# Layer 0 of a two-layer graph network: filter taps split four pairs at a time through device memory, one power for two roots, the gate kept in PSUM

## The reference

```
norm  = (sum(adj, -1) + 1e-6) ** -0.5
f_hom = norm * (adj @ (norm * (x @ theta)))
f_het = x @ W_h
gate  = sigmoid(x @ W_t + b_t)
x1    = layernorm(x + elu(gate * f_hom + (1 - gate) * f_het))
layer 1: conv1d(relu(bn(conv1d(x1, conv1_w))), conv2_w[256, 256, 17]), similarity message, GRU, layernorm
```

## Time and profile before

| | us |
|---|---|
| median of 3 runs (2112.98 to 2114.28) | 2113.04 |
| the profiled execution | 2112.74 |
| its span, first to last instruction | 2111.0 |
| `phase_a`: ends before the next phase's first instruction at | 541.60 |

### The profile page before, as it was taken

How to read it: one execution, slowest core, us unless ns; L and a number is a source line. 1 busy time by engine, 2 the same in 40 slices (tenths; PEclk the granted TensorE clock), 3 DMA queues, 4 the chain that set the end, 5 groups by cost and what they waited for, 6 DMA issues and landing times.

```text
span 2111.0 us, 36299 instructions
## 1 busy us (share of the span) xinstructions
PE 1916.6 (91%) x11046; PEld 1668.0 (79%) x11046; DVE 1551.1 (73%) x3024; ACT 1154.2 (55%) x2174; POOL 424.7 (20%) x374
## 2 busy tenths in 40 slices
PE   6888888888588879996699999999999999999997
PEld 5887777787588868885588888888888888888886
DVE  5998799898577767764577777777777777777774
ACT  6887688787355557664344444444444444444442
POOL 5887687686000000000000000000000000000000
PEclk9999999999699989998699999999999999999998
DMA  4565556565422238886212212121221212212110
GB/s 140 205 212 203 205 216 217 190 211 185 154 79 84 80 127 270 256 262 200 106 62 79 84 57 93 47 93 65 74 89 51 93 47 93 73 67 93 63 41 20
DMA packets 175099, 263.23 MB, mean 125 GB/s; under 512 B 13406, under 2 KB 125764, under 8 KB 170788
## 3 DMA queue, kind: packets, MB, share of 16 engines
q1 hardware_dynamic: 175012, 262.27, 36.7%
HBM read 174.14 MB, written 88.08 MB: 124 GB/s over the span
## 4 chain that ended last, share of the span: by engine, by line
PE 50%; issue 1%; DVE 1%; DMA 1%; SPq 0%; ACT 0%; POOLq 0%; POOL 0%; ACTq 0%; DVEq 0%
PE c_ps_g L1438 37%; PE c_ps_m L1416 4%; PE c_ps_m L1447 2%; PE c_ps_y L1473 1%; PE c_ps_m L1449 1%; PE c_ps_y L1531 1%; PE c_ps_m L1531 1%; PE c_ps_m L1448 1%; DMA c_yf<-y_spec 1%; PE c_ps_s L1516 0%; PE c_ps_y L1532 0%; PE c_ps_m L1532 0%; PE c_ps_s L1487 0%; PE c_ps_g L1490 0%; DVE c_wi_l L1381 0%
## 5 line engine op out<-in xcount | busy, mean ns | idle before, releaser
L1207 POOL TENSOR_TENSOR c_rstd<-c_var_eps,c_neg_half 128x4 f32<-128x4 f32 x32 | 32.2, 1007 | 1078.4 <-DVE c_var_eps L1345 1078.4
L1130 ACT ACTIVATE c_yo<-c_ps_y,c_shift,c_rstd 128x256 f32<-128x256 f32 x128 | 61.8, 563 | 170.0 <-DVE c_shift L1353 170.0
L1438 PE MATMUL c_ps_g<-c_ch,c_wi_l 128*128 128x512 f32 x384 | 154.6, 403 | 0.0
L1438 PE MATMUL c_ps_g<-c_nh,c_wi_l 128*128 128x512 f32 x384 | 153.3, 399 | 0.0
L837 PE MATMUL m_ps<-m_wh,m_xl 128*128 128x256 f32 (+1 forms) x406 | 132.9, 327 | 21.9 <-DVE m_wl L817 21.8
L1438 PE MATMUL c_ps_g<-c_xh,c_wh_l 128*128 128x512 f32 x384 | 152.1, 396 | 0.0
L1438 PE MATMUL c_ps_g<-c_xl,c_wh_h 128*128 128x512 f32 x384 | 152.0, 396 | 0.0
L1438 PE MATMUL c_ps_g<-c_xh,c_wh_h 128*128 128x512 f32 x384 | 151.7, 395 | 0.0
L1438 PE MATMUL c_ps_g<-c_ch,c_wi_h 128*128 128x512 f32 x384 | 151.6, 395 | 0.0
L1438 PE MATMUL c_ps_g<-c_cl,c_wi_h 128*128 128x512 f32 x384 | 151.6, 395 | 0.0
L1438 PE MATMUL c_ps_g<-c_nl,c_wi_h 128*128 128x512 f32 x384 | 151.2, 394 | 0.0
(11 more groups left out here) (225 smaller groups left out, 6403.8 us busy)
## 6 DMA issues: line engine op xcount, KB each, us to landing
w_spec<-a_spec SPq DMA_DIRECT2D x32, 1088.0 KB, 11.0
m_w<-w_spec SPq DMA_DIRECT2D x34, 1024.0 KB, 7.4
a_xt<-in_x_t SPq DMA_DIRECT2D x64, 256.0 KB
a_xn<-in_x_n SPq DMA_DIRECT2D x64, 256.0 KB, 9.5
x_t<-a_x1t SPq DMA_DIRECT2D x64, 256.0 KB, 9.8
s_x<-x_t SPq DMA_DIRECT2D x64, 256.0 KB, 3.0
y_spec<-m_y SPq DMA_DIRECT2D x64, 256.0 KB, 5.9
c_x<-x_t SPq DMA_DIRECT2D x32, 512.0 KB, 3.9
```

Source lines behind the costliest of these rows:

```text
L1130: nc.scalar.activation(yo[:, b], ps_y[:, b], ACT.Identity, bias=shift[:, b:b + 1], scale=rstd[:, b:b + 1]).then_inc(s_yo, 1)
L1207: nc.gpsimd.tensor_tensor(rstd[:, :], var_eps[:, :], neg_half[:, :], ALU.pow).then_inc(s_rstd, 1)
L1438: last = nc.tensor.matmul(out, stationary, moving, start=(count == 0), stop=(count == total - 1))
```

## The change

1. Taps. SP loads the taps of four pairs at once as a tile of 128 partitions (`tr`); ACT makes the high part `th` and DVE the low part `tl`, once in four steps. SP stores high, low and high to a new tensor in device memory, `taps_s`, and later loads for each pair one tile of 102 rows (`gs`, four buffers), already stacked. `gr`, `gh` and DVE's stacking go. The spectra of a pair are made four steps later than before (step q+6, the fourth one in q+7), and the quarters of `w_spec` are stored in steps n%8 = 1 to 4 and not 4 to 7; the last four follow the last step.
2. Roots. The sum of adj and the variance stand side by side in `sums_eps`, and POOL raises both to -0.5 in one instruction (`roots`). The addition of epsilon to the variance goes from ACT to DVE; `x1` becomes a `scalar_tensor_tensor` with the root broadcast as a second tensor.
3. Gate. The tanh is written back into `ps_g`; `gd` reads it there, and PE's next gate projection waits for `gd`. `mix` reads the second half of `ps_hh` and not `het`.
4. `xn` has four buffers; `res` stands ahead of `al` on POOL. On PE the projection of the first graph stands ahead of `ps_hom`. On DVE the statistics stand ahead of `diff`.
5. `phase_product` counts two semaphores in one.

```diff
 SP
-                    for copy in range(3):
-                        sp.dma_start(gr[copy * 2 * TAPS:(copy + 1) * 2 * TAPS, r].rearrange("p c k -> p (c k)"),
-                                     taps[:, bass.ts(i, 4 * P)]).then_inc(s_in[r], 16)
+                    if n % TB == 0:
+                        m = k * (UNROLL // TB) + n // TB
+                        reached(sp, s_tl, m)
+                        sp.dma_start(tr[:, :], here.rearrange("o p c -> (o p) c")).then_inc(s_tr, 16)
...
+                    if n % TB == 0:
+                        reached(sp, s_tl, m + 1)
+                        for copy, part in enumerate((th, tl, th)):
+                            sp.dma_start(here[:, copy].rearrange("o (p c) -> (o p) c", p=P), part[:, :].bitcast(F32)).then_inc(s_ts, 16)
+                if live(6):
+                    reached(sp, s_ts, 48 * (m + 1))
+                    sp.dma_start(gs[:, r].rearrange("p c k -> p (c k)").bitcast(F32),
+                                 here.rearrange("o h (r x c) -> (o h r) x c", x=TB, c=4 * P)[:, at_step]).then_inc(s_gs[r], 16)
-                piece = n % 8 - 4
-                if 0 <= piece < PIECES and live(5 + piece):
+                piece = n % 8 - 1
+                if 0 <= piece < PIECES and live(10 + piece):
 ACT
+                if live(7):
+                    spectra_out(i - 7, 3, 7)
...
-                    nc.scalar.activation(var_eps[:, :], mv[:, v, :, 1], ACT.Identity, bias=eps[:, 0:1]).then_inc(s_ve, 1)
-                    nc.scalar.activation(gate[:, u], ps_g[:, :, :], ACT.Tanh, scale=0.5).then_inc(s_gate, 1)
+                    nc.scalar.activation(ps_g[:, :, :], ps_g[:, :, :], ACT.Tanh, scale=0.5).then_inc(s_gate, 1)
 POOL
+                    nc.gpsimd.tensor_tensor(roots[:, u, these], sums_eps[:, u, these], neg_half[:, these], ALU.pow).then_inc(s_root, 1)
 DVE
-                    nc.vector.scalar_tensor_tensor(gd[:, :, :], gate[:, v], 1.0, diff[:, :, :], ALU.add, ALU.mult).then_inc(s_gd, 1)
+                    nc.vector.scalar_tensor_tensor(gd[:, :, :], ps_g[:, :, :], 1.0, diff[:, :, :], ALU.add, ALU.mult).then_inc(s_gd, 1)
-                        last = nc.vector.tensor_scalar(x1[:, u, b], y[:, u, b], mv[:, u, b, 0:1], rstd[:, u, b:b + 1],
+                        last = nc.vector.scalar_tensor_tensor(x1[:, u, b], y[:, u, b], mv[:, u, b, 0:1], roots[:, u, 2 + b:3 + b].to_broadcast([P, D]),
...
 PE
                 if live(2):
...
+                    project(0)
+                if live(7):
+                    spectra(i - 7, 3, 7)
...
-                    spectra(0)
-                    project(0)
-                    spectra(1)
+                if live(6):
+                    spectra(i - 6, 0, 6)
+                if live(2):
                     project(1)
...
-                    reached(pe, s_gate, p2)
+                    reached(pe, s_gd, p2)
```

More of the change, by code:

```diff
@@ L49, in pipeline, with phase_a @@
         step(i, i % unroll, i // unroll, lambda s, i=i: 0 <= i - s < units)
-def phase_a(nc, G, x_n, x_t, adj_t, w0, b_t, masks, x1_t, taps, dft_w, w_spec):
+def phase_a(nc, G, x_n, x_t, adj_t, w0, b_t, masks, x1_t, taps, taps_s, dft_w, w_spec):
     pairs = G // 2
@@ L130, in phase_a @@
         s_wl = sem("weights_low")
-        s_in = [sem(f"x_adj_taps_loaded{b}") for b in range(RING)]
-        s_xn = [sem("x_nodes_loaded0"), sem("x_nodes_loaded1")]
+        s_in = [sem(f"x_adj_loaded{b}") for b in range(RING)]
+        s_xn = [sem(f"x_nodes_loaded{b}") for b in range(RING)]
         s_xh = sem("x_high")
@@ L157, in phase_a @@
         s_ve = sem("var_eps_done")
-        s_rstd = sem("rstd_done")
         s_x1 = sem("x1_done")
-        s_tr = sem("transposed")
+        s_xp = sem("transposed")
         s_x1t = sem("x1t_copied")
         s_out = [sem("x1t_stored0"), sem("x1t_stored1")]
-        s_gh = sem("taps_high")
-        s_gs = sem("taps_stacked")
+        s_tr = sem("taps_loaded")
+        s_th = sem("taps_high")
+        s_tl = sem("taps_low")
+        s_ts = sem("taps_stored")
+        s_gs = [sem(f"taps_stacked{b}") for b in range(RING)]
         s_gm = sem("spectra_made")
@@ L364, in step @@
                     nc.vector.scalar_tensor_tensor(y[:, v], mix[:, v], 0.0, res[:, v], ALU.max, ALU.add).then_inc(s_y, 1)
-                if live(3):
-                    reached(dve, s_gd, p3)
-                    reached(dve, s_hom, p3 + 1)
-                    reached(dve, s_het, p3 + 1)
-                    for b in range(2):
-                        last = nc.vector.scalar_tensor_tensor(diff[:, b], ps_hom[:, b], norm[:, v, b:b + 1], het[:, v, b],
-                                                              ALU.mult, ALU.subtract)
-                    last.then_inc(s_diff, 1)
-                if live(5):
                     reached(dve, s_mv, p5)
@@ L390, in step @@
                 if live(3):
+                    reached(dve, s_gd, p3)
+                    reached(dve, s_hom, p3 + 1)
+                    reached(dve, s_het, p3 + 1)
+                    for b in range(2):
+                        last = nc.vector.scalar_tensor_tensor(diff[:, b], ps_hom[:, b], roots[:, v, b:b + 1], het[:, v, b],
+                                                              ALU.mult, ALU.subtract)
+                    last.then_inc(s_diff, 1)
+                if live(5):
+                    reached(dve, s_mv, p5 + 1)
+                    reached(dve, s_root, p5 + 3)
+                    nc.vector.scalar_tensor_tensor(sums_eps[:, v, 2:4], mv[:, v, :, 1], 1.0, eps[:, :], ALU.mult, ALU.add).then_inc(s_ve, 1)
@@ L486, in step @@
                     last.then_inc(s_gp, 1)
[L487 removed]
+                if live(6):
+                    spectra(i - 6, 2, 6)
             pipeline(pe, pairs, STAGES, step, unroll=UNROLL)
@@ L1647 @@
     y_n = nc.dram_tensor("out_y", (P, G * D), F32, kind="ExternalOutput").ap()
-    phase_a(nc, G, d["x_n"], d["x_t"], d["adj_t"], d["w0"], d["b_t"], d["masks"], x1_t, d["taps"], d["dft_w"], w_spec)
+    phase_a(nc, G, d["x_n"], d["x_t"], d["adj_t"], d["w0"], d["b_t"], d["masks"], x1_t, d["taps"], taps_s, d["dft_w"], w_spec)
     with ExitStack() as ctx:
```

196 lines of the change are left out of this document (98 added, 98 removed).

## The result

Median 2080.95 us (2077.3 to 2083.8, 4 runs) against 2113.66 (2112.98 to 2114.68, 4 runs): ratio 0.9844, 95% interval 0.9827 to 0.9861. The profiled execution took 2079.74 us, 33.0 less than before's 2112.74.

A forecast was written before the change was run, and what follows sets the result against it. It took two DMA engines loading the taps, then the engines' 7.55 us loop held by DVE, to bound the kernel. -5 - 5 - 44.6 - 1 + 15 = -40.6 took 2112.7 to 2072 us; range given 2048 to 2101.

The forecast's parts named there:

- start, to the gate of step 2: Kernel's beginning: ACT's first x no longer waits for the taps; -5 us (-3 to -7).
- steps 2 to 8: Six early steps of 7.15 us, four of them now without spectra, put at 6.3 each: -5 us (0 to -7).
- steps 8 to 63: Main stretch: 441.0 us becomes 55 x 7.0 + 11.4 = 396.4, so -44.6.
- steps 63 to 65: The last two steps take 14 us in place of 15.05: -1.
- end, to the next phase: Last four stores of spectra, 13.5 us in place of 4.3 (+9.2), and spectra through one buffer (+6): together +15.
- the step of 8.02: Mean step before, steps 8 to 63; explained by two DMA engines needing 6.5 us plain, 9.4 with a spectra store.
- The DMA sum of 8.0: Mean need per step of the two busiest DMA engines before: (6.5 + 9.4) / 2 = 8.0 us.
- the six engines that 102 rows were put at: Taps load at 17 rows to an engine: six DMA engines, 1.4 us; busiest engines then need 5.9 us a step.
- The rival of two engines: 102 rows still get two DMA engines: 8.7 us a step, main stretch 478.5, total 2155 us; chance 0.04.
- DVE falls off the path: Engines' loop of 7.55 us, held by DVE; edits change DVE's sum by -0.2 to -1.4 us, below what comes next.
- a ring of 7.0 us through ACT and PE: Gate, ACT's work and spectrum copy, then PE to the next gate: sum 6.9, taken as 7.0 us a step.
- The jumps back: Two loop ends where ACT's 4.27 us stall stays and PE's clock drops: 5.7 us each, 11.4 in all.

The follow-up runs named there:

- the two runs with the load's other form: Changed kernel with three loads of 34 rows: 2166.37 us, ratio 1.0259; kernel before with one load of 102 rows: 2088.66 us, ratio 0.9884.
- the extra operation: Changed kernel with one more 102x512 DVE operation in each step, the size of the removed `gs` stacking: 2080.84 us, ratio 0.9855.
- spectra off the ring: Changed kernel with PE's spectra and ACT's copies of them moved to where the buffer has long been free: 2075.92 us, ratio 0.9832.
- The runs with the start opened: Changed kernel, spectra moved, loop written out, PE's first step not waiting for `bt_rows`, 11 unneeded products ahead: 2052.12 us; also with two buffers for last three pairs' spectra: 2043.57.
- off the ring, no loop: Changed kernel with spectra and their copies moved to where the buffer is free, and all 64 steps written out: 2053.53 us, ratio 0.9729.
- stores two steps later: Changed kernel with the quarters of the spectra stored in steps n%8 = 3 to 6 in place of 1 to 4: 2077.42 us, ratio 0.9835.

## Why the prediction was right, and where it was off

By its own steps, in the profiled executions:

| step | predicted | measured |
|---|---|---|
| start, to the gate of step 2 | -5 | -1.0 (24.10, now 23.14) |
| steps 2 to 8 | -5 | -3.5 (42.90, now 39.37) |
| steps 8 to 63 | -44.6 | -40.8 (441.03, now 400.26) |
| steps 63 to 65 | -1 | -1.3 (15.05, now 13.74) |
| end, to the next phase | +15 | +16.9 (18.5, now 35.4) |
| the phases behind it | 0 | -3.7 (1569.4, now 1565.7) |
| sum | -40.6 | -33.4 |

The forecast of 2072 us was 9 too low, and by more in the part that changed: without the 3.7 us of the phases behind, which no run ties to the change, the gain would have been 29.7. That is luck on the forecast's side. So is a part of how the step of 8.02 was explained. The DMA sum of 8.0 contains no jump, but the measured mean does: 53 steps take 414.3 us, 7.82 each, with only eight of them over 9, and the two jumps 26.8. The cause named, the two engines, stands all the same by the two runs with the load's other form.

*The DMA engines* came out as worked out: the six engines that 102 rows were put at show in the share of 0.38 and held nothing up, while three loads of 34 rows behind the same stores did, in the same kernel. The rival of two engines (2155, with a main stretch of 478.5) was priced at about what that kernel then took (2166, 477.6).

*DVE falls off the path, and a ring of 7.0 us through ACT and PE comes next.* Both shown: the extra operation cost nothing, and spectra off the ring gave 6.82. The ring was the last to end by 0.16 us alone. Not shown is which edit took DVE off the path. PE's wait for `fl`, 0.84 us at a time before, is gone, and three things could have done it: the projection that now stands in front of `ps_hom`, the shorter `mix` and `gd`, and the `gs` that went. Only the last was put back by itself, and it didn't bring 7.55 back; no run undoes the order on PE or the operands in PSUM alone. `mix` at 688 ns is what the Trainium skill's "SBUF — State Buffer", section "Who interferes with whom", leads to for an operand moved to PSUM, and `gd` with 681 too; `x1`, which by that rule stays blocked, is not slower with its third input but faster than its 762, at 672. POOL's `res` fell as well, from 1724 to 1292 ns (60 to 215 us). But the prediction misread a row where it saw the rule confirmed: `gs`, with its 775 ns the unblocked one there, also has two SBUF inputs (`gh` and `gr`), and so has `y`, at 676 ns before and 688 after. Two inputs in SBUF don't make an operation slow by themselves, and no run moves one operand alone.

*The jumps back* were mis-sized: 11.4 for two, 15.7 measured. The step that failed was that the stall "stays". ACT's is the same, 4.46 us against 4.27 in the earlier trace rows, but DVE now stands twice. The timeline of the first jump:

```profile
228.59 0.16 DVE L379 TENSOR_SCALAR a_sums_eps<-a_ps_t 128x2 f32<-128x2 f32 x1 [4.61 <-issue]
228.95 0.63 ACT L269 ACTIVATE a_below<-a_mix 128x512 f32<-128x512 f32 x1 [4.46 <-issue]
...
233.88 0.18 DVE L392 BATCH_NORM_AGGREGATE a_mv<-a_stats 128x2 f32<-128x6 f32 x1 [3.25 <-issue]
```

The second jump is alike (4.51 and 3.15 on DVE). In the trace before DVE stood once, for 2.99 us in the first jump. The two jumps are 4.3 us over what was put down for them; the 53 other steps, (400.26 - 29.65) / 53 = 6.99 us each, give 0.4 of it back. That is all by which the main stretch missed. The runs show that the loop is what stalls, but not why DVE does so twice.

*The start* was the term furthest off. ACT did have its first x at 10.00, as said, but PE had something else to wait for, and then ran slowly. PE's first instruction in after, and two of its passes:

```profile
15.22 0.37 PE L472 MATMUL a_ps_t<-a_ones,a_al 128*128 128x2 f32 x1 [15.22 <-DVE a_bt_rows L370]
...
16.67 0.63 PE L463 MATMUL a_ps_hh<-a_w_lo,a_xh 128*128 128x512 f32 x1
...
21.29 0.39 PE L504 MATMUL a_ps_g<-a_bt_rows,a_ones 128*128 128x512 f32 x1
```

DVE's preparation of the weights ends in `bt_rows`, which nothing needs before the gate. The step to blame is that I followed ACT's wait and never asked what PE's first instruction waits for. Before, that was `al`, at 16.40, with `bt_rows` long done at 13.7; in after `bt_rows` itself ended only at 15.2, with DVE's `dw` at 1.50 us for 0.49 beside a POOL that now works at the same time. So PE began 1.2 us earlier, and not even that was kept whole: its passes became fast at 21.19 before and at 21.29 in after. The runs with the start opened give 2.2 us back, 4.5 where the passes were fast as well (gate at 19.47).

*Steps 2 to 8* were put at 6.3 us each. The four without spectra took that (6.25 to 6.35), the two with spectra 7.06 and 7.04: that is the missing 1.5.

*The end* was right in both terms. From the last copy of `x1t` at 497.50 the stores take to 511.90, where the next phase's first instruction stands:

```profile
497.50 0.60 ACT L305 ACTIVATE a_x1t<-a_ps_t 128x512 f32<-128x512 f32 x1 [0.45 <-PE a_ps_t L500]
...
511.90 0.20 POOL L597 MEMSET s_ones<- 128x128 f32 x1 [23.45 <-POOLq L66]
```

That is 13.8 us after the copy's end, predicted 13.5; the spectra back and forth took 7.4 more than before's tail, predicted 6.

*The phases behind* were put at 0. Their code is the same but for the semaphores merged in `phase_product`. With that merge they took 1561.4 us (off the ring, no loop) to 1569.0 (stores two steps later) in the profiled executions, without it 1567.7 (before with one load of 102 rows) and 1569.4 (before). The -3.7 lies within that spread; no run has the merge alone, so what it is worth stays open.

## What to carry to other kernels

Look at how many rows a small load has before how many bytes: in this kernel one load of 102 rows in place of three of 34 was worth 1.16% (22.3 us between the medians) without any other change, and undoing it turned the whole change into a loss. When a change frees an engine, ask at once for the next that ends last, here a ring only 0.16 us above PE's own passes, so that taking still more off DVE would have given nothing. Work that is deferred to shorten each step comes back at the end of the loop, uncovered (16.9 us here); a second buffer for the last pairs' spectra took 5.1 of it back. And a start is as early as the last thing that its first matmul waits for.

## What the runs showed of the hardware that I had not expected

- A jump back in this loop costs 7.0 and 8.7 us over a step in after, 2.0 and 3.6 in before with one load of 102 rows (9.56 and 11.13 for 7.55): ACT stands in "issue" for 2.2 to 4.5 us and DVE for 1.1 to 4.6, in after DVE twice (4.6 and 3.3, with 2.0 us of work between them). Written out, the same steps have no such stall, at 7.04 us a step for 6.98. With DVE's extra operation DVE stood only once, and the jumps cost 6.7 and 4.9 over a step. What sets the length of the stall stays open.
- The clock's column says 1.00 for the first microseconds of PE's work in after, as this window has it:

```profile
15.20:20.00 4.80, 4.78 (x13) 3.99 (x14) 0.76 (x2) 0.47 (x1) 2.66 (x3) 1.00 0.84 236
```

Yet its passes of 128x512 follow each other there at 0.43 us and from 21 us on at 0.23, near the 2 between the two levels of 1.2 and 2.4 GHz. In the tail the same column does say 0.50, from 485 us to the end of the phase. With unneeded products ahead from about 9.5 us on, one execution had its passes slow until 18.88 and another had them fast from the first, at 14.74. So the early work doesn't bring fast passes each time, and whether it did so that once isn't shown.
